# Row transposes of the late feed-forward blocks moved from TensorE to VectorE and DMA, with GpSimd drains behind each block

## The reference

```
x = x + xattn(layer_norm(ctx), layer_norm(x))        # keys and values from both, 16 heads, Wout
z = layernorm(x)
e = argmax(z @ centroids.T)                          # one of 8 experts per token
xn = layer_norm(z) * ln_g[e] + ln_b[e]
y = z + relu(xn @ w1[e].T + b1[e]) @ w2[e].T + b2[e]
a = sigmoid(z . centroids[e])
out = x + a * y + (1 - a) * z
```

## Time and profile before

| | us |
|---|---|
| median of 3 runs | 1091.27 |
| lowest and highest | 1089.54, 1091.30 |
| profiled execution, its time | 1091.64 |
| profiled execution, its span | 1089.8 |
| TensorE busy | 1063.2 |
| VectorE busy | 790.3 |
| ScalarE busy | 662.0 |
| GpSimd busy | 515.8 |

### The profile page before, as it was taken

One profiled execution on the slowest core, in us unless ns is written; L12 is line 12 of the kernel. 1 busy time (PEld: TensorE's weight loads), 2 busy tenths in 40 slices (PEclk: granted clock), 3 DMA queues, 4 the chain that ended last, 5 costly groups with the idle time before them and its releaser, 6 DMA issues.

```text
span 1089.8 us, 24096 instructions
## 1 busy us (share of the span) xinstructions
PE 1063.2 (98%) x8508; PEld 953.5 (87%) x8508; DVE 790.3 (73%) x1873; ACT 662.0 (61%) x1819; POOL 515.8 (47%) x640
## 2 busy tenths in 40 slices
PE   7899999999999999999999999999999999999995
PEld 6689888989888888989898888889898999999994
DVE  5786888888888988888887988888975543333331
ACT  4674766575756767665767667665665555555540
POOL 1563555546464555546464645555345533332331
PEclk9998999999999999999999999999999999999998
DMA  5465576765857566766758576765468466556540
GB/s 167 116 159 158 145 194 163 189 170 145 216 139 199 148 182 163 190 164 170 182 150 209 150 187 148 188 167 130 101 174 291 143 209 234 207 201 241 198 158 23
DMA packets 152172, 187.11 MB, mean 172 GB/s; under 512 B 16621, under 2 KB 141549, under 8 KB 147184
## 3 DMA queue, kind: packets, MB, share of 16 engines
q1 hardware_dynamic: 147600, 175.68, 58.7%
q0 software_dynamic: 3360, 8.53, 2.2%
q10 hardware_dynamic: 1088, 1.31, 0.3%
HBM read 65.72 MB, written 46.07 MB: 103 GB/s over the span
## 4 chain that ended last, share of the span: by engine, by line
PE 93%; DVE 2%; POOL 1%; DMA 1%; ACT 1%; issue 1%; SPq 0%; ACTq 0%; POOLq 0%; DVEq 0%
PE psum L661 16%; PE psum L694 15%; PE psum L836 12%; PE psum L731 11%; PE psum L821 10%; PE psum L710 9%; PE psum L746 9%; PE psum L680 8%; PE psum L749 1%; PE psum L789 1%; DMA w_ring<-in_w_q 1%; POOL prob L1583 1%; DMA prob_t<-prob 1%; DVE neg_max L1221 0%; POOL w_o_lo L1637 0%
## 5 line engine op out<-in xcount | busy, mean ns | idle before, releaser
L1583 POOL TENSOR_TENSOR prob<-prob,inv_sum 128x512 f32<-128x512 f32 x176 | 182.8, 1053 | 206.0 <-DVE inv_sum L1227 205.5
L990 ACT ACTIVATE prob<-psum,neg_max 128x256 f32<-128x256 f32 x352 | 164.3, 479 | 47.9 <-DVE neg_max L1221 40.4
L1221 DVE TENSOR_REDUCE neg_max<-psum 128x2 f32<-128x512 f32 x256 | 162.2, 673 | 34.9 <-PE psum L710 34.7
L836 PE MATMUL psum<-w,v_n 128*128 128x256 f32 x608 | 134.2, 379 | 0.0
L1233 DVE STREAM_TRANSPOSE prob<-prob 128x512 f32<-128x512 f32 x176 | 121.5, 699 | 9.5 <-POOL prob L1583 8.9
L836 PEld LDWEIGHTS psum<-w,v_n 128*128 128x128 f32 x608 | 114.1, 190 | 14.8
L1654 POOL DMA_INDIRECT out<-x_in,r_ring x38 | 47.5, 1250 | 152.2 <-DVE x_in L1452 146.4
L1583 POOL TENSOR_TENSOR w_ring<-w_ring,inv_sum 128x512 f32<-128x512 f32 x76 | 78.2, 1042 | 78.0 <-DVE inv_sum L1227 77.7
L997 ACT ACTIVATE head_out_hi<-psum 128x512 fp32r<-128x512 f32 x52 | 31.1, 598 | 114.6 <-PE psum L731 107.7
L969 ACT ACTIVATE k_hi<-psum 128x512 fp32r<-128x512 f32 x128 | 77.2, 603 | 22.9 <-PE psum L661 19.3
L980 ACT ACTIVATE v_n<-psum 128x512 f32<-128x512 f32 x128 | 78.2, 611 | 20.9 <-PE psum L694 20.9
(11 more groups left out here) (183 smaller groups left out, 2712.1 us busy)
## 6 DMA issues: line engine op xcount, KB each, us to landing
sorted_rows<-filler SPq DMA_DIRECT2D x54, 660.0 KB, 5.0
prob_t<-prob SPq DMA_DIRECT2D x176, 128.0 KB, 2.8
w_ring<-prob SPq DMA_DIRECT2D x176, 128.0 KB
w<-in_experts SPq DMA_DIRECT2D x19, 1024.0 KB
w_ring<-in_experts SPq DMA_DIRECT2D x18, 1024.0 KB, 6.0
prob_t<-w_ring SPq DMA_DIRECT2D x76, 128.0 KB, 2.8
w_ring<-w_ring SPq DMA_DIRECT2D x76, 128.0 KB
w_ring<-normed SPq DMA_DIRECT2D x56, 128.0 KB, 3.0
```

What stands on the lines that cost most here:

```text
L836: last = pe.matmul(bank[:, i * d_model:(i + 1) * d_model], hid[:, s % 2, f, i * P:(i + 1) * P], w2[:, f * d_model:(f + 1) * d_model], star ...
L990: act.activation(prob_at(u, bb)[:, :, parity, i], scores_i, ACT.Exp, bias=neg_max[:, at, i:i + 1], accum_out=prob_sum[:, at, i:i + 1]).the ...
L1221: dve.tensor_reduce(neg_max[:, (4 * u + n) % 8, :], psum[:, n, :].rearrange("p (i j) -> p i j", i=2), AXIS_X, ALU.max, negate=True).then_i ...
L1583: pool.tensor_tensor(probs, probs, inverse, ALU.mult).then_inc(s_soft, 1)
```

## The change

- For blocks 6 and later `row_transposes` is gone. `normalise_rows` writes the rows in the permuted order (`row_blocks`), VectorE transposes them in place in 32x32 blocks (`transpose_rows`, one instruction of 128x512, at the head of its round), SP's queue moves them with four DMAs of 128 partitions by 128 columns into `x_cols` (`move_rows`, behind the loads of its round, waiting for the transpose and for the gain and bias of the block before), and `row_gain_bias` reads `x_cols`.
- Each half of the second layer has its own bank and its own signal; `finish` and the waits go by halves. `bank_order` has four numbers for each late block, two of which ("pass") stand for banks that are left out.
- GpSimd waits after each late block for the landing of both halves and executes a DRAIN, as it does once ahead of them. Its late blocks are nested in conditions, a block within that of the one before, and the eight conditional waits at the end are gone.

The diff, cut to its core (lines that stay are left out, indentation is reduced):

```
@@ -67,10 +69,11 @@
-order += [("rank", n_pairs - 2), ("ft", 1), ("fy", 0), ("pv", n_steps - 1), ("wout", n - 2), ("ft", 2), ("wout", n - 1)]
-order += [("ft", 3), ("fy", 1), ("rank", n_pairs - 1), ("total",), ("ft", 4), ("fy", 2)]
+order += [("rank", n_pairs - 2), ("ft", 1), ("fy", 0, 0), ("fy", 0, 1), ("pv", n_steps - 1), ("wout", n - 2), ("ft", 2), ("wout", n - 1)]
+order += [("ft", 3), ("fy", 1, 0), ("fy", 1, 1), ("rank", n_pairs - 1), ("total",), ("ft", 4),
+          ("fy", 2, 0), ("fy", 2, 1)]
...
-    order += [("ft", slot + 2)] * (slot + 2 < n_slots) + [("fy", slot)]
+    order += [("ft", slot + 2) if slot + 2 < n_early else ("pass", slot, 0), ("fy", slot, 0), ("fy", slot, 1), ("pass", slot, 1)]
@@ -287,6 +293,9 @@
+row_blocks = normed[:].rearrange("p (s i) (j c k) -> p s (i j c k)", s=2, i=2, j=4, c=KC).rearrange(
+    "p s (j i c k) -> p s j i c k", j=4, i=2, c=KC)
+row_cols = x_cols[:].rearrange("p b c t -> p (b c t)").rearrange("p (a i c t) -> p a i c t", a=4, i=2, c=KC)
@@ -351,7 +360,7 @@
-        eng.wait_ge(f_y, item[1] + 1)
+        eng.wait_ge(f_y, 2 * item[1] + item[2] + 1)
@@ -470,7 +483,7 @@
-        wait_made(sp, ("fy", s - NW2))
+        wait_made(sp, ("fy", s - NW2, 1))
@@ -497,6 +510,18 @@
+def move_rows(s):
...
+    sp.wait_ge(f_xt, s - n_early + 1)
+    if s == n_early:
+        wait_made(sp, ("wout", n_batches - 1))
+    else:
+        sp.wait_ge(f_g, s - n_early)
+    for a in range(4):
+        sp.dma_start(row_cols[:, a].rearrange("p i c t -> p (i c t)"),
+                     row_blocks[a * Q:(a + 1) * Q, s % 2].rearrange("p j i c t -> p j (i c t)")
+                     ).then_inc(f_xm[s % 2], 16)
@@ -596,6 +621,7 @@
+    run(s, (move_rows,))
@@ -604,6 +630,8 @@
+    while order[made[0]][0] == "pass":
+        made[0] += 1
@@ -823,20 +851,20 @@
-    bank = begin(("fy", s))
...
+        bank = begin(("fy", s, i))
...
-            last = pe.matmul(bank[:, i * d_model:(i + 1) * d_model], hid[:, s % 2, f, i * P:(i + 1) * P],
+            last = pe.matmul(bank[:, 0:d_model], hid[:, s % 2, f, i * P:(i + 1) * P],
...
-    last.then_inc(f_y, 1)
+        last.then_inc(f_y, 1)
@@ -912,12 +940,12 @@
-    row_transposes(s + 2)
+    if s + 2 < n_early:
+        row_transposes(s + 2)
...
-    run(s + 2, (row_transposes,))
@@ -1030,17 +1058,26 @@
+    elif s < n_early + 2:
+        wait_made(act, ("ft", s - 2))
...
-        wait_made(act, ("ft", s - 2))
+        wait_rows_moved(act, s - 2)
...
-        last = act.activation(xhat[:, s % 2, i, :], row[:, 0:d_model], ACT.Identity,
+        src, dst = row[:, 0:d_model], xhat[:, s % 2, i, :]
+        if s >= n_early:
+            src = src.rearrange("p (c k j) -> p j c k", c=KC, j=4)
+            dst = row_blocks[:, s % 2, :, i]
+        last = act.activation(dst, src, ACT.Identity,
...
-    wait_made(act, item)
+    if s < n_early:
+        wait_made(act, item)
+    else:
+        wait_rows_moved(act, s)
@@ -1048,16 +1085,23 @@
-        last = act.activation(xn[:, c, :], work_bank(number[item])[:, c * BLOCK:(c + 1) * BLOCK], ACT.Identity,
-                              bias=vec[:, KC + c:KC + c + 1], scale=vec[:, c:c + 1])
-    last_reads(item, last)
+        if s < n_early:
+            src, dst = work_bank(number[item])[:, c * BLOCK:(c + 1) * BLOCK], xn[:, c, :]
+        else:
+            src = row_cols[:, :, :, c, :].rearrange("p a i t -> p i a t")
+            dst = xn[:, c, :].rearrange("p (i a t) -> p i a t", i=2, a=4)
+        last = act.activation(dst, src, ACT.Identity, bias=vec[:, KC + c:KC + c + 1], scale=vec[:, c:c + 1])
+    if s < n_early:
+        last_reads(item, last)
+    else:
+        last.then_inc(f_g, 1)
...
-        wait_made(act, ("fy", s - 2))
+        wait_made(act, ("fy", s - 2, 1))
@@ -1421,8 +1465,17 @@
+def transpose_rows(s):
...
+    dve.wait_ge(f_xh, s + 1)
+    rows = xhat[:, s % 2].rearrange("p i d -> p (i d)")
+    dve.transpose(rows, rows).then_inc(f_xt, 1)
...
-    wait_read(dve, ("ft", s))
+    if s < n_early:
+        wait_read(dve, ("ft", s))
+    else:
+        dve.wait_ge(f_g, s - n_early + 1)
@@ -1435,20 +1488,21 @@
-    item = ("fy", s)
-    wait_made(dve, item)
...
-    last_reads(item, dve.tensor_tensor(upd, work_bank(number[item]).rearrange("p (i d) -> p i d", i=2),
-                                      b2_ring[:, s % NR, None, :].to_broadcast([P, 2, d_model]), ALU.add))
-    dve.wait_ge(f_base, s + 1)
-    if s >= 2:
-        dve.wait_ge(f_out[s % 2], 32 * (s // 2))
-    wait_read(dve, item)
...
+        item = ("fy", s, i)
+        wait_made(dve, item)
+        last_reads(item, dve.tensor_tensor(upd[:, i, :], work_bank(number[item])[:, 0:d_model],
+                                          b2_ring[:, s % NR, :], ALU.add))
+        if i == 0:
+            dve.wait_ge(f_base, s + 1)
+            if s >= 2:
+                dve.wait_ge(f_out[s % 2], 32 * (s // 2))
+        wait_read(dve, item)
@@ -1560,12 +1614,14 @@
+    if s + 2 >= n_early:
+        transpose_rows(s + 2)
...
-    run(s + 2, (low_weights_1,), (split_xn,))
+    run(s + 2, (transpose_rows,), (low_weights_1,), (split_xn,))
@@ -1702,14 +1758,17 @@
-for s in range(n_early, n_slots):
-    run(s + 2, (add_base,))
-    run(s, (write_rows,))
...
-for s in range(n_sure - 1, n_slots):
-    with pool.If(empty == n_slots - 1 - s):
-        for i in range(2):
-            pool.wait_ge(f_out[(s - i) % 2], 32 * ((s - i) // 2 + 1))
+pool.wait_ge(f_out[(n_early - 2) % 2], 32 * ((n_early - 2) // 2 + 1))
+pool.wait_ge(f_out[(n_early - 1) % 2], 32 * ((n_early - 1) // 2 + 1))
+pool.drain()
+with ExitStack() as inner_blocks:
+    for s in range(n_early, n_slots):
+        if s >= n_sure:
+            inner_blocks.enter_context(pool.If(empty < n_slots - s))
+        run(s + 2, (add_base,))
+        write_rows(s)
+        pool.wait_ge(f_out[s % 2], 32 * (s // 2 + 1))
+        pool.drain()
```

More of the change, by code:

```diff
@@ L35, with bank_order @@
 NW, NW2, NR = 2, 3, 4
-def bank_order(n_pairs, last_of_early, n_slots):
+def bank_order(n_pairs, last_of_early, n_early, n_slots):
     n_steps = 4 * n_pairs
@@ L121, in build @@
     assert 5 <= n_early <= n_sure - 2
-    order = bank_order(n_pairs, last_of_early, n_slots)
+    order = bank_order(n_pairs, last_of_early, n_early, n_slots)
     number = {item: i for i, item in enumerate(order)}
@@ L265, in build @@
             f_xh = sem("f_xh")
+            f_xt = sem("f_xt")
+            f_xm = [sem("f_xm0"), sem("f_xm1")]
+            f_g = sem("f_g")
             f_base = sem("f_base")
@@ L408, in wait_inputs_moved, with wait_rows_moved @@
                 eng.wait_ge(s_moved[g % 2], 4 * 16 * (g // 2))
+            def wait_rows_moved(eng, s):
+                eng.wait_ge(f_xm[s % 2], 4 * 16 * ((s - n_early) // 2 + 1))
             def wait_high(eng, g, side):
```

## The result

| us | before | changed |
|---|---|---|
| median of 4 runs | 1090.4 | 1075.24 |
| lowest and highest | 1088.03, 1091.3 | 1074.57, 1076.51 |
| profiled execution, its time and span | 1091.64, 1089.8 | 1074.92, 1073.1 |

A forecast was written before the change was run, and what follows sets the result against it. TensorE bounds the late blocks, with a GpSimd tail behind its last matmul. 5.7 + 1.55 + 0.5 + 5.3 = 13.0 us (13.05) off gave 1078.3 us for the median, range 1076.8 to 1085.5, chance 0.84.

The forecast's parts named there:

- Term 1: Late blocks 6 to 18: row transposes leave TensorE, 0.44 us a block in 13 blocks, 5.7 us saved.
- the rival of a partial overlap: Between first and second layer: transposes' 0.44 us is partly overlap; with nothing given back 1084.0 us, chance 0.04.
- Term 2: Behind the last matmul: second layer in halves, half 0 finished and written earlier, 1.55 us saved.
- Terms 3 and 4: GpSimd's end: nested conditions leave fewer branches, 0.5 us; added DRAINs shorten the exposed DRAIN time, 5.3 us.
- The reading of the DRAIN: GpSimd's DRAINs: 0.080 us per DMA since the last DRAIN; first added 3.7 us, a block's 0.33, final 0.17.
- Both rivals with full prices: GpSimd's DRAIN: full price once after any DMAs, 1083.7 us, chance 0.16; both end DRAINs full, 1089.3 us, 0.06.
- The chain of the moves: Late rounds: VectorE's transpose, SP's four moves, ScalarE's gain and bias, in time for TensorE's next first layer.
- the spare: Late rounds: 2.2 to 3.7 us between the last move's landing and the latest landing that TensorE allows.
- The limit for the weights' copy: Late rounds: the second layer would wait if ScalarE's weights copy ended later than 4.9 us behind the round's start.
- the base of the sum: Whole kernel: 13.0 us taken off the profiled 1091.64 us and the median of 1091.27, giving 1078.6 and 1078.3.

The follow-up runs named there:

- the folded kernel: Changed kernel with b2 times alpha plus base computed ahead of the second layer: 1076.37 and 1075.69 us, ratio 0.9875 twice to the kernel before.

## Why the prediction was right about the change and wrong about the time

- **Term 1**, 5.7 us: 5.64, in the whole change and alone. The chain's 0.44 us a block was all given back; the rival of a partial overlap is out.
- **Term 2**, 1.55 us: 1.63 in the change, 1.54 alone. The last write ends 2.75 us behind the last matmul (2.83 forecast).
- **Terms 3 and 4**, 0.5 and 5.3 us: 6.1 together. The reading of the DRAIN as a price for each GpSimd DMA since the last one holds at five counts. Its constant was too high: a block's is 0.20 (0.33 forecast), the final one 0.046 (0.17), since I took the preamble's 174 ns for it, which a DRAIN with no DMA behind it doesn't cost at the end. Both rivals with full prices are out. The Trainium skill's 12 ns for the DRAINs of preamble and postamble (VectorE: DVE Perf Modes, The DRAIN you can't avoid) agrees with SP, ScalarE and VectorE at 13, 8 and 17 ns in the changed kernel, and not with GpSimd, 46 to 5797 ns. In the folded kernel VectorE's took 57 ns.
- **The chain of the moves**: right in order, transpose and moves 0.2 to 0.3 us earlier than laid out. The weights were asked for at T + 7.3 instead of T + 6.7 in the round shown and up to T + 9.8 in others; the forecast had read one of the earliest rounds of before. The slowest landing was 4.7 us, where 4.3 was taken as the worst. ScalarE's gain and bias did wait for the DMA in 3 rounds of 13, where none was expected. It cost nothing, by the spare.
- **The limit for the weights' copy**, T + 4.9, was wrong, without effect on the sum. In the round from 884.11 the copy starts at 888.03 and takes 1.91, so it ends at T + 5.8, and no second layer waited. The relus behind it are read by a second layer one round later, because each round ends with `layer_2` of the block before.
- **The step that failed is the base of the sum**: "it lies 0.37 above the median of 1091.27. So 1078.6 in a profiled execution like it, 1078.3 for the median". Three runs of 1089.54 to 1091.30 stood for the kernel, and one trace for its first stage. In 29 later runs it had 1085.58 to 1092.76, median 1089.22 (1088.57 and 1090.0 in 9 and 15 runs on two other chips), and the trace had the latest first stage of all 14. From 1089.22 the measured 13.4 us lead to 1075.8; the changed kernel measured 1075.24, 1075.70 and 1076.96. The forecast's own range, 1077 to 1080, held the doubt of the terms, and nothing for the first 800 us, which differ by 1.7 to 2.3 us between traces of the same program. The prediction names 2.2 us as what a measurement of this kernel can tell, but has no such term in its sum or its range. With a low end 2 us lower the range would have held the time.

## What to carry to other kernels

Forecast a change as a difference between fixed points of the program, and put the spread of executions of the same program into the range as a term of its own: here the sum over the change's stages was right within 0.4 us, while the stage ahead of them moved by 4.3 over the traces. GpSimd's DRAIN at the end has a price for each of its DMAs; where the engine has time and its DMAs have landed, drain behind each piece of work and the end has only the last piece's. A transpose that is exposed on the bound engine can go over VectorE and four moves; here that cost TensorE nothing, and still nothing with the moves issued 2.7 us later, but 1.5 us in all with 4.2. Measure such a spare by holding the issue back.

## What the runs showed of the hardware

- Behind work, GpSimd's DRAIN took 0.046 us and 0.082 more for each DMA (of 128 rows) that GpSimd had issued since its last DRAIN, though all had landed: 0 to 70 DMAs, 46 to 5797 ns. The one of the preamble, with no DMA before it, took 174 ns.
- Between 82 and 93 us every trace has some us of half the clock (1.2 GHz) with TensorE busy: 3 to 4 us in seven traces, about 7 in the other seven, and those are 1.5 us slower there.
- The last write of 128 rows lands 1.44 us after its issue ends in all traces but two, which have 1.88 and 1.97 and an instruction fetch in that stretch.
- The same program compared with itself gave a ratio of 0.9987 with an interval of 0.9976 to 0.9999, which leaves out 1. About 0.2% is what a comparison like these can't be trusted with; the moves alone fell short of their stages by about as much.
